# The program's block is opened without the drain of GpSimd at its end

## The chip, the cores and the metric

The kernel runs on one core of one Trainium2 chip. A core has five engines with instruction streams of their own: TensorE (PE), VectorE (DVE), ScalarE (ACT), GpSimd (POOL) and SyncE (SP). They meet only at semaphores. Sixteen DMA engines move data between HBM and the on-chip memory; here they are fed from the queues of SP, ACT and POOL. The metric is the device time of one execution in microseconds (us), lower is better.

## What is computed

The reference is two layers of a graph network on 50,000 nodes of 128 features with 12,500 edges. Cut to what matters:

```
# layer 0: max over the edges that enter a node
e      = x[src] * (1 + softplus(c) * edge_weight)
pooled = relu(layer_norm(e @ pool_w + pool_b))
agg    = max(segment_max(pooled, dst), 0)
h      = relu(layer_norm(concat(x, agg) @ final_w + final_b))
x      = layernorm(x + h)
# layer 1: relational convolution, 8 bases, mean over the edges
msg    = x[src];  coeff = comp[edge_type]
agg_b  = segment_sum(msg * coeff[:, b], dst) / max(deg, 1)     # b = 0..7
out    = concat(agg_0..agg_7, x) @ weight + bias
x      = layernorm(x + out)                                     # the result
```

## The kernel before

The edges are sorted by destination and padded to 98 tiles of 128. The nodes are worked on in 98 groups of 4 x 128 rows, then 25 further groups take up the nodes that have edges. Two loops, unrolled, run on all engines.

The first loop (`step`, up to about 645 us of the trace) makes the dense part of both layers. SP loads and stores whole groups; GpSimd adds a bias row (L436), gathers source and destination rows by index, scales the source rows, and in its last part scatters the corrected rows of layer 0 into the table `x1_table` (L406 and L413 are the helpers `indirect` and `gather`, which issue all indirect DMAs).

The second loop (`step_c`, 25 units of up to four edge tiles) makes the edge part of layer 1: GpSimd gathers four tiles of rows, TensorE and VectorE form the products and segment sums, ScalarE scales the result (L810), and GpSimd scatters it into the output, 98 indirect DMAs in all. A unit's scatters are issued five units behind its gather (`OUT_LAG`), so the last five units of GpSimd's stream hold no gathers, only scatters. After the loop GpSimd waits until all scatters have landed (L493 and L494: one wait for each of the four semaphores `out_scattered`). These are its last instructions inside its body.

The order of the instructions is that of the code; no scheduler moves anything.

Of the kernel before, what the change touches and what calls it, by code (L numbers as in the profile page):

```python
# [71 lines left out]
def gnn_kernel(nc, x, src_cols, dst_cols, dst_next_cols, dst_rows, dst_prev_rows, type_line,  # L72
# [34 lines left out]
    with ExitStack() as ctx:  # L107
# [166 lines left out]

            return x1[:, g % 2, m, :] if g < DENSE else agg_all[:, (g - DENSE) * CH + m, :]

        block = ctx.enter_context(nc.Block())  # L277

        @block.sync  # L280
# [1003 lines left out]
```

How the kernel before makes its waits and increments, by code:

```python
def need(eng, sem, count):  # L47
    if isinstance(count, int) and count <= 0:
        return
    eng.wait_ge(sem, count)
# [13 lines left out]
    def need(self, at):  # L65
        self.eng.wait_ge(self.sem, at)
# [239 lines left out]
            def coef_load(q):  # L306
                r = q * PAIR // (TYPE_TILES * LINE_BLOCKS)
                sp.wait_ge(line_stored[r], 16 * len(blocks_of(r)))
                used = q - COEF_SLOTS
                if used >= 0:
                    sp.wait_ge(S["dve_prod"], products_upto(used * PAIR // UNIT, 1, used % (UNIT // PAIR)))
                sp.dma_start(coefs[:, q % COEF_SLOTS, :, :, :].rearrange("p t b e -> p (t b e)"),
                             coef_line[q * PAIR:(q + 1) * PAIR].rearrange("(o t) b e -> o (t b e)", o=1)
                             .broadcast_to([P, PAIR * NB * P])).then_inc(coefs_in[q % COEF_SLOTS], 16)
# [1 line left out]
            def step(s):  # L316
                c = s
                b = c % 2
                if c == 2:
                    sp.wait_ge(S["mask_made"], 1)
                    sp.dma_start(mask_line.rearrange("o (t e) -> (o t) e", e=P), same_rows[:, :]).then_inc(S["mask_stored"], 16)
                if c == 4:
                    sp.wait_ge(S["mask_stored"], 16)
# [6 lines left out]
                    t = c - LATE  # L330
                    slot = t % SLOTS
                    sp.wait_ge(dst_in[slot], 16 * (t // SLOTS + 1))
                    sp.dma_start(x_dst_table[:, bass.ds(t * D, D)], x_dst[:, slot, :]).then_inc(dst_stored[slot], 16)
```

## Time and profile before

| | us |
|---|---|
| median of three runs | 912.48 (911.65 to 912.67) |
| the profiled execution, its own time | 910.83 |
| its span, first to last instruction of the program | 909.0 |
| GpSimd busy | 717.8 |
| TensorE, VectorE, ScalarE busy | 769.2, 777.6, 610.0 |

The profile is of one execution. Its page gives busy time by engine, the span in 40 slices (each digit tenths of a slice), the DMA queues, and the chain of work that ended last.
### The profile page before, as it was taken

Reading aid. Unit: us, or ns where it says so; the run is one execution under the profiler, and the core shown is the slowest. Engines: PE = TensorE matmul, PEld = TensorE weight load, DVE = VectorE, ACT = ScalarE, POOL = GpSimd, SP = SyncE. Lnnn points to the kernel's source line nnn. Section 1 sums busy time; section 2 is a strip of 40 time slices with the busy share of each in tenths; the row PEclk is TensorE's granted clock in tenths of the full one; section 3 lists DMA queues with packets and bytes.
Section 4 is the critical chain, followed back from the end, with each engine's and each line's share of the span. In section 5 each row is a group of like instructions: output and inputs, shape, how many; then the busy total and the mean of one; then the engine's idle time right before and its main releaser. Section 6 shows DMA issues by size and latency. Waiting matters only on the chain. (4 is left out here: it accounts for less than half of the span.)

```text
span 909.0 us, 18559 instructions
## 1 busy us (share of the span) xinstructions
PE 769.2 (85%) x4588; PEld 566.3 (62%) x4588; DVE 777.6 (86%) x2823; ACT 610.0 (67%) x2862; POOL 717.8 (79%) x702
## 2 busy tenths in 40 slices
PE   5699999999999999999999988777299998988920
PEld 3577777777777777777778777666144444444410
DVE  6889999999999999999999979887179999989940
ACT  3799999999999999999999867776201111111120
POOL 2588888988989898898898667777777777777774
PEclk9999999999999999999999989999799999999975
DMA  4377676666666666666666422334188888877610
GB/s 114 111 230 236 193 234 209 197 213 206 207 199 215 205 201 207 208 205 198 203 205 200 123 67 86 101 107 177 46 293 272 304 295 286 300 276 286 230 47 27
DMA packets 88576, 175.46 MB, mean 193 GB/s; under 512 B 16716, under 2 KB 34024, under 8 KB 82199
## 3 DMA queue, kind: packets, MB, share of 16 engines
q1 hardware_dynamic: 71286, 144.02, 46.7%
q0 software_dynamic: 15744, 29.71, 10.8%
q8 instruction: 38, 0.62, 0.3%
q10 hardware_dynamic: 1440, 0.56, 0.2%
q14 instruction: 68, 0.55, 0.2%
HBM read 105.88 MB, written 70.88 MB: 194 GB/s over the span
## 5 line engine op out<-in xcount | busy, mean ns | idle before, releaser
L704 ACT ACTIVATE junk<-ps 128x128 bf16<-128x128 f32 x884 | 235.1, 301 | 30.1 <-PE ps L554 19.3
L704 ACT ACTIVATION_READ_ACCUMULATOR junk<-ps 128x1 f32 x884 | 206.7, 235 | 0.0
L656 PE MATMUL ps<-agg_all,w_cen 128*128 128x512 f32 (+1 forms) x400 | 176.0, 593 | 5.9 <-DVE agg_all L1185 5.1
L406 POOL DMA_INDIRECT x_dst<-in_x,dst_i x98 | 153.9, 1571 | 17.6 <-issue 7.7
L551 PE MATMUL ps<-w_cen,xT 128*128 128x128 f32 x984 | 160.2, 295 | 0.0
L436 POOL TENSOR_TENSOR work<-work,vec_raw 128x512 f32<-128x512 f32 x98 | 127.8, 1304 | 30.4 <-DVE work L1084 29.7
L551 PEld LDWEIGHTS ps<-w_cen,xT 128*128 128x128 f32 x984 | 129.9, 197 | 28.9 <-issue 28.9
L1185 DVE TENSOR_TENSOR agg_all<-coefs,ps 128x1024 f32<-128x1024 f32 x98 | 117.7, 1210 | 31.6 <-PE ps L642 18.3
L1084 DVE SCALAR_TENSOR_TENSOR work<-ps,st,vec_raw 128x128 f32<-128x128 f32 x492 | 137.8, 343 | 0.4 <-ACT st L719 0.3
L1016 DVE BATCH_NORM_STATS2 bn<-work 128x6 f32<-128x128 f32 x492 | 135.2, 280 | 1.2 <-DVE st L1004 0.6
L406 POOL DMA_INDIRECT x_table<-agg_all,scat_i x98 | 104.9, 1070 | 37.7 <-issue 28.3
L524 PE MATMUL ps<-w_cen,work 128*128 128x128 f32 x984 | 132.5, 279 | 0.0
L656 PEld LDWEIGHTS ps<-agg_all,w_cen 128*128 128x128 f32 x400 | 75.2, 193 | 91.3 <-issue 90.9
L743 ACT ACTIVATE work<-work,st 128x128 f32<-128x128 f32 x294 | 126.4, 525 | 0.6 <-DVE st L1072 0.6
L524 PEld LDWEIGHTS ps<-w_cen,work 128*128 128x128 f32 x984 | 122.1, 195 | 0.1
L406 POOL DMA_INDIRECT out_rows<-work,scat_i x98 | 97.4, 994 | 29.9 <-issue 29.2
L413 POOL DMA_INDIRECT rows<-in_x,src_i x98 | 95.4, 973 | 29.9 <-issue 29.6
L413 POOL DMA_INDIRECT rows<-x_table,src_i x98 | 93.5, 954 | 31.8 <-issue 29.6
L805 ACT ACTIVATE st<-st 128x4 f32<-128x4 f32 x25 | 5.1, 205 | 163.4 <-DVE st L1221 163.1
L537 PE MATMUL ps<-ident,rows 128*128 128x128 f32 x590 | 89.1, 282 | 19.4 <-ACT xT L764 8.7
L537 PEld LDWEIGHTS ps<-ident,rows 128*128 128x128 f32 x590 | 70.4, 146 | 24.3 <-ACT xT L764 11.0
L1030 DVE SCALAR_TENSOR_TENSOR work<-work,rows 128x512 f32<-128x512 f32 x123 | 84.6, 688 | 0.0
(139 smaller groups left out, 1371.9 us busy)
## 6 DMA issues: line engine op xcount, KB each, us to landing
coefs<-coef_line SPq DMA_DIRECT2D x49, 1024.0 KB, 6.0
rows<-in_x SPq DMA_DIRECT2D x97, 256.0 KB
x_table<-work SPq DMA_DIRECT2D x97, 256.0 KB
out_rows<-outb SPq DMA_DIRECT2D x97, 256.0 KB
x_dst_table<-x_dst SPq DMA_DIRECT2D x98, 64.0 KB
rows<-x_dst_table SPq DMA_DIRECT2D x24, 256.0 KB
same_prev<-mask_line SPq DMA_DIRECT2D x7, 224.0 KB, 4.1
x_dst<-in_x,dst_i POOLq DMA_INDIRECT x98, 4.0
```

The source lines that it names most:

```text
L406: return pool.indirect_dma_start(*args, bounds_check=last_node, oob_is_err=False)
L413: return pool.indirect_dma_start(rows_of, None, table, by(columns, t))
L436: pool.tensor_tensor(h, h, vec_raw[:, BET_F:BET_F + 1, :].broadcast_to([P, CH, D]), ALU.add).then_inc(S["pool_b"], 1)
L524: last = pe.matmul(Y[b][:, cols(m, m + 1)], x1T[:, b, m, :], w_cen[:, W_ROOT, :], start=True, stop=True, skip_group_check=True)
L537: last = pe.transpose(XT[:, cols(m, m + 1)], rows[:, slot, m, :], ident[:, :])
L551: last = pe.matmul(H[1 - b][:, cols(m, m + 1)], xT[:, 1 - b, m, :], w_cen[:, W_TOP, :], start=False, stop=is_dense(c, 1), skip_group_check ...
L656: last = pe.matmul(MT[b][:, 0:n * D], w_cen[:, W_BASE + m, :], prod[:, b, m, 0:n, :].rearrange("p t d -> p (t d)"), start=(m == 0), stop=( ...
L704: last = nc.scalar.activation(junk[:, kind * CH + m, :], bank[:, cols(m, m + 1)], ACT.Square, accum_out=power[:, b, 1, TOP + kind * CH + m ...
L743: last = nc.scalar.activation(x1_tile(c - 4, m), hn[:, (c - 4) % SLOTS, m, :], ACT.Identity, bias=st[:, 3, TOP + m:TOP + m + 1], scale=st[ ...
L1016: own.mark(dve.bn_stats(bn[:, RES + m, :], hn[:, (c - 3) % SLOTS, m, :]))
L1084: last = dve.scalar_tensor_tensor(hn[:, (c - 2) % SLOTS, m, :], H[b][:, cols(m, m + 1)], st[:, 7, TOP + m:TOP + m + 1], vec_raw[:, GAM_F, ...
L1185: dve.tensor_tensor(prod[:, b, half, two, :], coefs[:, p % COEF_SLOTS, :, half, :].rearrange("p t m d -> p m t d"), GX[c % len(GX)][:, col ...
```

## The change

The block is opened with a flag that leaves the DRAIN of GpSimd out of the barrier at its end.

```
-        block = ctx.enter_context(nc.Block())
+        block = ctx.enter_context(nc.Block(no_gpsimd_drain=True))
```

No instruction in the five bodies changes, and none changes its place. In the barrier behind them, by the instructions of the two programs:

- GpSimd: the DRAIN is gone. What is left is the EVENT_SEMAPHORE that waits until `gather` is 4 and the one that sets `release`.
- TensorE, VectorE, ScalarE, SP: the DRAIN stays but signals nothing; behind it stands one more EVENT_SEMAPHORE each, which adds one to `gather`, and then the wait for `release` as before.

The barrier ahead of the bodies keeps all its DRAINs. The waits at L494 stay.

## Rows read from the trace of the kernel before

**Rows 1.** The page: span, busy time by engine, the span in 40 slices.

```profile
span 909.0 us, 18559 instructions
...
PE 769.2 (85%) x4588; PEld 566.3 (62%) x4588; DVE 777.6 (86%) x2823; ACT 610.0 (67%) x2862; POOL 717.8 (79%) x702
...
POOL 2588888988989898898898667777777777777774
PEclk9999999999999999999999989999799999999975
DMA  4377676666666666666666422334188888877610
```

**Rows 2.** Busy time by stretch (us from start to end, length, busy by engine; clock, DMA).

```profile
core 0: us, PE busy (x) PEld busy (x) DVE busy (x) ACT busy (x) POOL busy (x), PEclk, DMA share, GB/s
693.00:850.00 157.00, 144.79 (x429) 70.21 (x428) 150.32 (x333) 26.91 (x91) 119.60 (x123) 0.99 0.82 292
850.00:880.00 30.00, 19.79 (x68) 11.13 (x68) 21.33 (x69) 7.41 (x25) 23.00 (x24) 0.90 0.29 102
880.00:899.90 19.90, 0.00 (x0) 0.00 (x0) 0.00 (x0) 0.69 (x2) 14.29 (x15) 0.50 0.14 45
899.90:909.00 9.10, 0.00 (x0) 0.00 (x0) 0.00 (x0) 0.00 (x0) 0.00 (x0) 0.50 0.00 0
```

**Rows 3.** Chain that ended last, 893 to 910 us: start, length, what.

```profile
894.69 0.30 issue
894.99 0.98 POOL out_rows L406
895.98 0.30 issue
...
897.31 0.26 issue
897.57 0.98 POOL out_rows L406
```

**Rows 4.** Scatters to the output from 880 us on: duration ns, starts, issue to landing.

```profile
L406 POOL DMA_INDIRECT out_rows<-work,scat_i x15: 982/982/984, 879.6 to 897.6; - x15
...
DMA to landing us min/median/max: 2.2/2.3/2.3
```

**Rows 5.** Source line L107, closing barrier: duration ns min/median/max, first and last start us.

```profile
L107 POOLq EVENT_SEMAPHORE  x2: 17/17/17, 908.9 to 908.9; - x2
L107 SPq DRAIN  x1: 128/128/128, 848.6 to 848.6; - x1
L107 PEldq DRAIN  x1: 487/487/487, 870.1 to 870.1; - x1
L107 DVEq DRAIN  x1: 203/203/203, 874.7 to 874.7; - x1
L107 ACTq DRAIN  x1: 674/674/674, 881.9 to 881.9; - x1
L107 POOLq COMPARE_BRANCH  x1: 41/41/41, 899.8 to 899.8; - x1
L107 POOLq DRAIN  x1: 8887/8887/8887, 899.9 to 899.9; - x1
L107 SPq EVENT_SEMAPHORE  x1: 17/17/17, 909.0 to 909.0; - x1
...
L107 PEldq EVENT_SEMAPHORE  x1: 51/51/51, 909.0 to 909.0; - x1
```

**Rows 6.** Source line L1273, opening barrier, same columns.

```profile
L1273 POOLq DRAIN  x1: 187/187/187, 0.3 to 0.3; - x1
...
L1273 SPq EVENT_SEMAPHORE  x1: 17/17/17, 0.7 to 0.7; - x1
```

**Rows 7.** Timeline of the start: start us, length, engine, line, operation, tiles.

```profile
1.29 0.73 POOL L385 DMA_DIRECT2D src_i<-in_src_cols  x1 [0.84 <-POOLq L1273]
...
4.24 0.29 POOL L399 TENSOR_SCALAR_AFFINE_SELECT ident<-pooled 128x128 f32<-128x128 f32 x1 [0.17 <-POOL rel_row L396]
...
5.20 0.71 PEld L537 LDWEIGHTS ps<-ident,rows 128*128 128x128 f32 x4 [5.20 <-POOL ident L399]
```

## The prediction

> **What bounds the kernel now.** I read the page first, then the end of the trace by stretches, then the chain, then the line of the closing barrier. The page shows three engines with much work over the span (VectorE 86%, TensorE 85%, GpSimd 79%), and GpSimd's row alone keeps its digits to the last slice [rows 1]. For a change that touches only the end of the program the averages say little; what matters is who comes last. The stretches say it: up to 850 us all of them work, between 880.0 and 899.9 us TensorE and VectorE do nothing, ScalarE has 0.69 us, and GpSimd has 15 scatters; from 899.9 to 909.0 us every engine has 0.00 us busy and the DMA engines move 0 GB/s [rows 2]. The chain gives the same order: GpSimd issues one scatter after another, 0.98 us each with 0.30 us of issue between them, the last from 897.57 us on [rows 3].
>
> The chain stops at 898.55 us (897.57 + 0.98), yet the span is 909.0 us. The 10.4 us between are of the kind that the chain leaves out, a sequencer's own. The view of line L107 has them [rows 5]: GpSimd's branch out of its body at 899.8, its DRAIN from 899.9 with 8887 ns, its two EVENT_SEMAPHOREs at 908.9, and the releases of the other engines at 909.0. The other four had come to their DRAINs between 848.6 and 881.9 us and been done after 674 ns at the most, so nobody is waited for but GpSimd. Two things bound the last 30 us, then: first GpSimd's issue of scatters, and behind it one DRAIN of 8.89 us that stands alone on the path.
>
> What does this DRAIN wait for? Not for data: the scatters land 2.2 to 2.3 us after their issue [rows 4], so the last has landed at about 897.57 + 2.2 = 899.8 us, and it is this landing for which L494 had GpSimd wait before the branch. Nor, as far as rows can tell, for a backlog of descriptors that GpSimd still had to write: then landings would fall behind the issues more and more, and over 15 scatters in a row they stay between 2.2 and 2.3 us. It is work, or polling, that the profile doesn't resolve. The DRAIN in the opening barrier, with four small memsets before it and no DMA, took 187 ns [rows 6].
>
> **The change part by part.**
>
> *The DRAIN of GpSimd goes.* 1 x 8.887 us [rows 5], alone on the path. Once it is gone, the next thing late is still GpSimd: its EVENT_SEMAPHORE finds the four arrivals in `gather` long made (the latest, ScalarE's, at 881.9 + 0.67 = 882.6 us, 17.3 us before), sets the release, and the others follow within 0.1 us, as they do now between 908.9 and 909.0. Bound from both sides: -8.89 us if nothing behind takes the work over, 0 if all of it comes back outside the program (first rival), and a gain beyond 8.89 us has no row for it, since the EVENT_SEMAPHOREs stay.
>
> *The other four engines get one EVENT_SEMAPHORE more each.* Such instructions take 17 ns on SP, 51 ns on TensorE [rows 5]. They lie at 849 to 883 us under the scatters of GpSimd, which run until 899.9 us. Cost nothing; the cover is 17 us thick. If it were gone, the dearest, ScalarE's or TensorE's, would add 0.02 to 0.05 us.
>
> *GpSimd's waits at L494* stay, so the output has landed before the barrier in both versions. The branch at 899.8 us stays as well.
>
> *The rest of the trace*, all up to 899.9 us, has the same instructions in the same order: cost 0. Runs differ by themselves (911.65 to 912.67 us, so -0.83 and +0.19 around the median).
>
> Sum, against the profiled execution: span 909.0 - 8.89 = 900.15 us, own time 910.83 - 8.89 = **901.94 us**. That execution lies 1.65 us under the median of the three runs, so for the median I take the same difference: 912.48 - 8.89 = **903.59 us**, that is -0.97%.
>
> The point that the sum rests on is what the time counts outside the span. The profiled execution's time is 1.83 us longer than its span (910.83 - 909.0), so something around the program is counted, at its start or at its end, and no row shows what. Of 8.89 us of another flush there is no room in it now, but before the change GpSimd has just been flushed when the program ends.
>
> On this the Trainium skill has a rule that speaks against the change. "VectorE: DVE Perf Modes", section "The DRAIN you can't avoid", says that the runtime puts DRAINs of its own before and behind a program, on all five engines, about 12 ns each. By this a DRAIN of GpSimd would follow the program anyway, and one that is 12 ns behind a flushed GpSimd need not be so behind one that is not; taken so, the sum would be 0 instead of -8.89 us. No row here shows an instruction outside the program. "Runtime: NRT & Kernel Launch", section "The ~15µs preamble/postamble breakdown", gives about 1.5 us to the barrier behind a program and 1.5 us to the reset of semaphores; 1.83 us of this trace is of that size, so part of it may be counted.
>
> **The rivals.**
>
> *The flush moves behind the program (no change).* What GpSimd has to finish after its indirect DMAs is finished at the point where somebody next needs the engine empty. If that is part of what follows the program and the time counts it, the DRAIN's 8.89 us come back there; some of it can run beside what lies in the 1.83 us. Time: 912.48 - 8.89 + 8.89 = 912.48, down to 910.7 if all of the 1.83 us hides it. For it: the DRAIN waits for neither data nor a backlog, which looks like a fixed duty that somebody must do; the time does count more than the span. Against it: 1.83 us is little, and that an ending needs the engine empty is shown nowhere; the DRAIN may be such a duty only because it is asked for. The same result would come if the flush fell to the next execution's opening DRAIN (187 ns now): GpSimd makes `ident` at 4.24 us, for which the first weight load waits until 5.20 us [rows 7], so 8.7 us there would be on the path in full.
>
> *It moves in part.* The work runs by itself from 899.9 us, and what comes behind meets only the rest, or only one half of the flush is needed: between 905 and 910 us, middle 907.5.
>
> *It is paid twice (slower).* If more than one point outside asks GpSimd to be empty, one behind the program and one at its start, and each finds the queue unflushed, each pays 8.89 us: 912.48 - 8.89 + 2 x 8.89 = 921.4 us. It decides from the second payment on; with one it is the rival above. Against it: an engine that has been flushed once answers a second time quickly, as the 1.83 us after the present DRAIN show, so the second would need new work in between, and there is none but the next execution's memsets.
>
> *The flag does nothing.* Excluded: the two programs differ by exactly this DRAIN and the four semaphore instructions.
>
> **How the numbers follow.** The forecast with the full gain: 0.62. It has the one row that is as plain as a row can be, an 8.9 us instruction alone on the path at the very end. The flush moved whole: 0.27, since the only doubt is outside the trace, and the trace gives the DRAIN nothing to wait for that would go away by itself. In part: 0.06. Twice: 0.05, with any other way to be slower.
>
> The predicted time is that of the likeliest, 903.6 us; its own range is 902.7 to 904.3 us (the spread of the runs on both sides, and 0.5 us for the barrier's new form). With 0.62 this is not yet 8 in 10, so the range reaches to the case of no change with its spread: 902.6 to 912.8 us, 0.62 + 0.27 + 0.06, less what falls over the edges, some 0.85; it can't be narrower, as the two cases lie at its ends. A measurement of this kernel tells 0.2% (1.8 us) from no change. Faster: 0.62 + 0.06 and a few of the moved case in which the 1.83 us hide it, less what is lost, makes 0.68. Within 0.2%: 0.26. Slower: 0.06.
>
> **What would show it.** In the changed kernel's profile, line L107 has no DRAIN of GpSimd, two EVENT_SEMAPHOREs of GpSimd at 899.9 to 900.1 us, and the releases of the other four at about 900.1; the span is 900.0 to 900.3 us. This part is close to certain (if everything up to 899.9 us repeats). What decides is the execution's own time against its span: 1.8 us more, as now, for the forecast; about 10.7 us more for the first rival with the flush at the end; and for a flush at the start a DRAIN at L1273 of some 9 us in place of 187 ns, and a span that is again 909. The prediction would be wrong as a whole if the time stayed at 912 with a span of 900, and wrong in its reading of the DRAIN if anything before 899.9 us moved.

## The result and the profile after

| | kernel before | changed kernel |
|---|---|---|
| median of four runs, us | 912.58 (911.65 to 914.93) | 903.98 (900.03 to 904.34) |
| ratio, with its 95% interval | | 0.9889 (0.986 to 0.9918) |
| the profiled execution: own time, span | 910.83, 909.0 | 903.88, 902.1 |

The change makes the kernel faster by 1.1% (0.8 to 1.4). The median came out at 903.98 us where 903.6 was forecast; the ratio says a little more than that, 0.9889 x 912.48 = 902.35 us, which lies 0.25 us under the lower end of the range. The section on where the prediction was right and where it failed comes back to it.

First the view of the closing barrier's line in the changed kernel, which answers to [rows 5] (columns: duration in ns min/median/max, first and last start in us):

```profile
L107 SPq EVENT_SEMAPHORE  x2: 17/17/17, 852.4 to 902.0; - x2
L107 PEldq EVENT_SEMAPHORE  x2: 51/51/51, 872.4 to 902.0; - x2
...
L107 ACTq EVENT_SEMAPHORE  x2: 17/17/17, 884.6 to 902.0; - x2
L107 POOLq EVENT_SEMAPHORE  x2: 17/17/17, 901.9 to 902.0; - x2
...
L107 ACTq DRAIN  x1: 686/686/686, 883.9 to 883.9; - x1
L107 POOLq COMPARE_BRANCH  x1: 41/41/41, 901.7 to 901.7; - x1
```

GpSimd has no DRAIN, and its EVENT_SEMAPHOREs stand 0.2 us behind its branch, where before 9.1 us lay between them (899.8 and 908.9). The four other engines have two EVENT_SEMAPHOREs each: the first, added one at 852 to 885 us, under the scatters of GpSimd; the second with the release at 902.0. What was to be seen at the start is there too; line L1273, as in [rows 6]:

```profile
L1273 POOLq DRAIN  x1: 187/187/187, 0.3 to 0.3; - x1
```

Busy time by stretch of the changed kernel, as in [rows 2]; the idle stretch of 9.1 us has become one of 0.4:

```profile
core 0: us, PE busy (x) PEld busy (x) DVE busy (x) ACT busy (x) POOL busy (x), PEclk, DMA share, GB/s
880.00:901.70 21.70, 0.00 (x0) 0.00 (x0) 0.00 (x0) 0.90 (x3) 15.72 (x16) 0.50 0.14 47
901.70:902.10 0.40, 0.00 (x0) 0.00 (x0) 0.00 (x0) 0.00 (x0) 0.00 (x0) 0.50 0.00 0
```

The end of the chain of the changed kernel, as in [rows 3] (start, length, what):

```profile
899.29 0.26 issue
899.55 0.98 POOL out_rows L406
```

The last scatter starts 2.0 us later than before (897.57), with the same instructions ahead of it. So this pair of profiled executions shows 6.9 us less span: 8.9 us from the DRAIN and 2.0 us lost in the body. Where the body lost them is told by the first gather of the second loop, line L413, before and after:

```profile
L413 POOL DMA_INDIRECT rows<-x_table,src_i x98: 940/945/982, 648.2 to 853.8; - x98
```

```profile
L413 POOL DMA_INDIRECT rows<-x_table,src_i x98: 940/945/982, 650.2 to 855.8; - x98
```

From this gather to the last scatter it is 249.4 us before (648.2 to 897.57) and 249.3 us after (650.2 to 899.55). The second loop repeats to 0.1 us, and the 2.0 us lie in the first loop.

The own time is 1.8 us over the span in both (910.83 - 909.0; 903.88 - 902.1), so nothing came back outside the program. This doesn't rest on one execution of each: over all executions of this and the later runs on chips where the kernel before takes about 912 us, the own time is 1.74 to 1.85 us over the span in 87 with the DRAIN, and 1.73 to 1.83 us in the 22 of the changed kernel.

### The profile page after: what moved, and what is told of

Same layout as the page of the kernel before. It is cut to its first block and busy times, and to the rows that moved or that the text cites. A ratio compares the mean times of both kernels' runs of the same rounds, so it can differ in the third digit from the quotient of the medians.

```text
span 902.1 us, 18562 instructions
## 1 busy us (share of the span) xinstructions
PE 771.0 (85%) x4588; PEld 566.9 (63%) x4588; DVE 779.1 (86%) x2823; ACT 609.9 (68%) x2862; POOL 713.0 (79%) x702
## 5 line engine op out<-in xcount | busy, mean ns | idle before, releaser
L656 PE MATMUL ps<-agg_all,w_cen 128*128 128x512 f32 (+1 forms) x400 | 179.0, 602 | 1.5 <-DVE agg_all L1185 0.9
L406 POOL DMA_INDIRECT x_dst<-in_x,dst_i x98 | 150.8, 1539 | 20.5 <-issue 7.1
L413 POOL DMA_INDIRECT rows<-in_x,src_i x98 | 95.5, 975 | 29.9 <-issue 29.6
L413 POOL DMA_INDIRECT rows<-x_table,src_i x98 | 93.5, 954 | 31.8 <-issue 29.2
```

What stands on the lines that cost most here:

```text
L406: return pool.indirect_dma_start(*args, bounds_check=last_node, oob_is_err=False)
L413: return pool.indirect_dma_start(rows_of, None, table, by(columns, t))
L656: last = pe.matmul(MT[b][:, 0:n * D], w_cen[:, W_BASE + m, :], prod[:, b, m, 0:n, :].rearrange("p t d -> p (t d)"), start=(m == 0), stop=( ...
```

## The experiments

All of them use the kernel before or the changed one with a line or two more. A DRAIN of GpSimd can be written by hand, `pool.drain()`, and has then a source line of its own.

### Is the DRAIN the whole effect?

**e1_after_again**: the changed kernel, unchanged.

> The changed kernel once more, unchanged. Theory A (the DRAIN's 8.89 us is the whole gain; what the first measurement showed beyond it, a ratio of 0.9889 or -10.1 us, is scatter of the first loop): ratio 0.9903, 8.9 us less, and the body (the start of GpSimd's branch at L107) at 899.8 us give or take 3 us, as before. Theory B (the missing DRAIN changes the body of the next execution too, by 1 us or more either way): ratio 0.989 or less, or 0.992 or more, with the branch shifted the same way in every profile without the DRAIN.

Measured: ratio 0.9885 (0.9862 to 0.9908), six runs with a median of 902.19 us. The profile's own time is again 1.8 us over its span (903.28, 901.5). The gain repeats, with theory A's 0.9903 inside the interval and B's value too. B's second condition, a shift of the body the same way in every profile, is not met: the second loop's first gather starts 2.0 and 1.2 us later than before in the first two profiles of the changed kernel (650.2, 649.4 against 648.2), and in the third, e9, 2.0 us earlier (646.2).

**e2_own_drain**: the flag stays, the DRAIN comes back by hand.

```
                 pool.wait_ge(out_scattered[j], 16 * sum(...))
+            pool.drain()
```

> The changed kernel with one DRAIN of GpSimd written out as the last instruction of its body, behind the wait for the scatters; the block's flag stays. If the DRAIN is the whole gain (A): the DRAIN takes 8.9 us, ratio to the kernel before 1.000, and the four added semaphore instructions cost nothing. If the gain came from the new form of the barrier, its waits or its signals (C): a ratio of 0.990, or a DRAIN well under 8.9 us.

Measured: ratio 0.9989 (0.9967 to 1.0011). The row of the line with the DRAIN in this kernel:

```profile
L495 POOLq DRAIN  x1: 8884/8884/8884, 898.1 to 898.1; - x1
```

With the flag and a DRAIN the gain is gone, so it is the DRAIN and not the barrier's form that makes it.

### What a DRAIN pays for

**e3_second_drain**: the kernel before with the same line added, so that two DRAINs stand in a row.

> The kernel before with a second DRAIN of GpSimd directly ahead of the block's own. If the DRAIN finishes something that is left over from the DMAs (D): the first takes 8.9 us, the second under 0.3 us, the time is 912.6. If a DRAIN has a fixed price once DMAs have been issued in the program (F): both take 8.9 us, the time is 921.4.

The two rows, of L495 and of the block's own at L107; one execution, 912.96 us:

```profile
L495 POOLq DRAIN  x1: 8884/8884/8884, 902.0 to 902.0; - x1
```

```profile
L107 POOLq DRAIN  x1: 40/40/40, 910.9 to 910.9; - x1
```

The second takes 40 ns. A DRAIN is not dear as such; it pays for something that the DMAs left and that is gone afterwards. Inside the program, then, whoever asks first pays and the next finds nothing, which speaks against the rival of a double payment.

**e4_many_drains**: the kernel before with DRAINs at five more places (the comments are added here).

```
+            pool.drain()                      # after the two index loads
             last_node = pool.to_reg(N - 1)
...
                 b = s % 2
+                if s in (10, 30):
+                    pool.drain()
...
+            pool.drain()                      # between the loops
             def gather_x1(q):
...
                 pool.wait_ge(out_scattered[j], 16 * sum(...))
+            pool.drain()
```

> The kernel before with DRAINs of GpSimd at five more places: behind the two plain loads at the start (landed), at steps 10 and 30 of the first loop, between the loops (all scatters landed; 242 indirect DMAs after the one before), and directly ahead of the block's own. If the price goes by the DMAs since the last DRAIN (D, 8887 ns for 490 indirect ones, 18 ns each): about 0.1 us, 0.2, 0.9, 4.4, 3.6 us and under 0.3 us for the block's own. If it is one price for any DRAIN with DMAs since the last (G): 8.9 us at each of the first five, under 0.3 us at the last. If it is a price per DRAIN (F): 8.9 us at all six. The time grows by what they sum to, less what the slack of GpSimd in the first loop hides.

The rows of GpSimd's DRAINs, from five source lines; the third line holds steps 10 and 30:

```profile
L402 POOLq DRAIN  x1: 223/223/223, 7.7 to 7.7; - x1
```

```profile
L433 POOLq DRAIN  x2: 5657/7250/8843, 48.9 to 149.4; - x2
```

```profile
L474 POOLq DRAIN  x1: 8619/8619/8619, 656.5 to 656.5; - x1
```

```profile
L499 POOLq DRAIN  x1: 8857/8857/8857, 917.4 to 917.4; - x1
```

```profile
L107 POOLq DRAIN  x1: 46/46/46, 926.3 to 926.3; - x1
```

None of the three theories holds. It is no fixed price (0.22 and 0.05 us exist), and it is not in proportion (244 DMAs cost 8.62 us, 196 cost 8.86; in the order of the program it is 244 since the DRAIN at step 30, all of them indirect, where the expectation says 242). The two inside the first loop can't be read as a price. GpSimd still worked on instructions ahead of them: its last one ended at 52.3 us under the DRAIN from 48.9 to 54.6, and at 154.2 us under the one from 149.4 to 158.2. What is left behind these ends, 2.3 and 4.0 us after 10 and 40 DMAs, can still hold the landing of the last transfers, which no row separates (timeline of GpSimd: start us, length, line, operation):

```profile
51.88 0.41 POOL L428 TENSOR_TENSOR rows<-rows,e_scale 128x128 f32<-128x128 f32 x1
54.62 1.27 POOL L439 TENSOR_TENSOR work<-work,vec_raw 128x512 f32<-128x512 f32 x1 [2.32 <-DVE work L1089]
```

So the 0.57 us a DMA that the next expectation takes from the 5.66 us is not a price.

**e5_late_drain** and **e6_idle_drain**: is it a backlog that GpSimd would work off by itself, or does the DRAIN start the work? In the first a long memset lies between the last landing and the DRAIN, in the second GpSimd waits idle for three loads of SyncE. Neither changes the result; both write buffers that are no longer read.

```
+            pool.memset(agg_all[:, 0:TILES, :], 0.0).then_inc(S["const_ready"], 1)
+            pool.wait_ge(S["const_ready"], N_CONST + 1)
+            pool.drain()
```

> The changed kernel with a memset of 128x12544 on GpSimd after all scatters have landed, then a wait for it, then a DRAIN of GpSimd. The memset overwrites a buffer nobody reads again. If the DRAIN ends something that GpSimd's cores are still busy with from the last DMAs (backlog, H): the memset starts some 8.9 us late or the DRAIN behind it takes under 0.3 us. If the DRAIN itself starts the work (I): the memset starts within 0.3 us of the branch-free end of the waits, and the DRAIN behind it takes 8.9 us.

```
+            pool.wait_ge(coefs_in[0], 16 * (len(range(0, PAIRS, COEF_SLOTS)) + 3))
+            pool.drain()
```

> The changed kernel with three loads of 1 MB on SyncE's queue, one after the other, once all scatters have landed; GpSimd waits idle for the last of them and then has a DRAIN. The loads fill a buffer nobody reads again. Backlog (H): the DRAIN, some 15 us after the last landing, takes under 0.3 us. Work started by the DRAIN (I): 8.9 us whatever the time between.

These two and the next two ran on another chip, where the kernel before took 979.6 us instead of 912, so only durations inside their traces are used. The timeline of GpSimd in e5 and the DRAIN behind it:

```profile
971.22 0.98 POOL L406 DMA_INDIRECT out_rows<-work,scat_i  x1 [0.30 <-DMA out_rows<-work,scat_i]
973.43 10.55 POOL L495 MEMSET agg_all<- 128x12544 f32 x1 [1.22 <-DMA out_rows<-work,scat_i]
```

```profile
L497 POOLq DRAIN  x1: 8884/8884/8884, 984.0 to 984.0; - x1
```

The memset starts 2.2 us after the last scatter's issue, that is with its landing [rows 4]: no backlog is ahead of it. And a DRAIN 10.6 us later takes the same 8884 ns. In e6, the last scatter, which lands at about 969.8 + 2.2 = 972.0 us, and the DRAIN 13.6 us behind that:

```profile
969.79 0.98 POOL L413 DMA_INDIRECT out_rows<-work,scat_i  x1 [0.30 <-DMA out_rows<-work,scat_i]
```

```profile
L503 POOLq DRAIN  x1: 8884/8884/8884, 985.6 to 985.6; - x1
```

The backlog falls. Waiting does nothing to the price, so what the DRAIN does begins with the DRAIN; left out, it is not done in the time that is measured.

**e7_counted_a**, **e8_counted_b**, **e10_counted_c**, **e11_counted_d**, **e12_counted_e**: the changed kernel with DRAINs after chosen counts of scatters, each behind waits until the scatters so far have landed. The edit shown is that of e7 and e8; e10, e11 and e12 also wait there for the gathers, and e12 has a DRAIN between the loops too.

```
+                        if done * UNIT + n + 1 in DRAIN_AT:
+                            for j in range(SLOTS):
+                                need(pool, out_scattered[j], 16 * ...)
+                            pool.drain()
```

> The changed kernel with DRAINs of GpSimd in the last 18 scatters, each behind a wait until all scatters so far have landed: after scatter 80 (hundreds of DMAs before it), then 1, 2, 4 and 11 DMAs after the DRAIN before. Price by DMA with a ceiling (10 DMAs gave 5.66 us at the start, 0.57 us each; 8.9 us for 16 or more): 8.9, 0.6, 1.1, 2.3 and 6.2 us. A price for any DRAIN with DMAs since the last (G): 8.9 us five times.

> The same with DRAINs after scatters 80, 86 and 98, so 6 and 12 DMAs after the DRAIN before. Price by DMA with a ceiling: 8.9, 3.4 and 6.8 us. One price (G): 8.9 us three times.

> The changed kernel with DRAINs of GpSimd in the second loop, each behind waits until all its DMAs so far have landed: after 336 DMAs, then after 16, 32, 48 and 60 more. By 40 ns and 82 ns a DMA since the last DRAIN (1 to 12 DMAs fit it): 1.35, 2.66, 3.98 and 4.96 us; the first near the ceiling, 7.4 to 8.9 us. If the line bends before 60: less.

> The same with DRAINs after 336 DMAs, then 120 and 36 more. By the line: 36 gives 2.99 us and 120 would give 9.9 us. If there is a ceiling at about 8.9 us (no measured DRAIN is above it): 8.9 us or less for 120.

> The same with DRAINs between the loops (296 DMAs), after 40 more and after 156 more. By the line 40 gives 3.32 us. By a ceiling 296 and 156 give 7.4 to 8.9 us; by a count that starts again at zero after each 128 DMAs, 3.3 and 2.3 us.

The rows of single DRAINs, each from the line's view over a stretch that holds one. From e7, after 1, 2, 4 and 11 DMAs since the one before:

```profile
L495 POOLq DRAIN  x1: 124/124/124, 957.4 to 957.4; - x1
```

```profile
L495 POOLq DRAIN  x1: 198/198/198, 961.8 to 961.8; - x1
```

```profile
L495 POOLq DRAIN  x1: 371/371/371, 968.9 to 968.9; - x1
```

```profile
L495 POOLq DRAIN  x1: 936/936/936, 985.1 to 985.1; - x1
```

From e10, the first DRAIN (336 DMAs), then those after 32 and 60 more; from e11, after 120 more; from e12, after 156 more:

```profile
L497 POOLq DRAIN  x1: 4474/4474/4474, 708.0 to 708.0; - x1
```

```profile
L497 POOLq DRAIN  x1: 2651/2651/2651, 783.9 to 783.9; - x1
```

```profile
L497 POOLq DRAIN  x1: 4937/4937/4937, 935.4 to 935.4; - x1
```

```profile
L497 POOLq DRAIN  x1: 2656/2656/2656, 865.3 to 865.3; - x1
```

```profile
L498 POOLq DRAIN  x1: 5591/5591/5591, 916.9 to 916.9; - x1
```

All DRAINs that stood behind landed DMAs, but for e4's first (223 ns behind the two plain index loads), in one table (GpSimd issues 492 DMAs, 490 indirect and the two index loads; the last column is the duration less 43 ns, by 81.6 ns, which is the slope between 1 and 60 DMAs: (4937 - 124) / 59):

| DMAs since the DRAIN before | DRAIN, ns | as DMAs |
|---|---|---|
| 1, 2, 4, 6 | 124, 198, 371, 533 | 1, 2, 4, 6 |
| 11, 12, 16 | 936, 1017, 1349 | 11, 12, 16 |
| 32, 36, 40 | 2651, 2977, 3309 | 32, 36, 40 |
| 48, 60 | 3957, 4937 | 48, 60 |
| 120 | 2656 | 32 |
| 156 | 5591 | 68 |
| 196 (e4) | 8857 | 108 |
| 244 (e4), 296 (e12) | 8619, 8639 | 105, 105 |
| 336 (e10, e11) | 4474 | 54 |
| 474 (e7, e8) | 7414 | 90 |
| 492 (the kernel before; e2, e3, e5, e6, e15) | 8887; 8884 in each | 108 |

How the expectations did: the one price of 8.9 us (G) and the ceiling with 0.57 us a DMA, of e7 and e8, are both wrong from 1 to 12 DMAs. The line of 40 ns and 82 ns a DMA, read from these, hit all six values from 16 to 60 that e10, e11 and e12 forecast by it, to 0.03 us, and failed at 120 (2.66 us for 9.9). The ceiling missed for 336 (4.47 us where 7.4 to 8.9 were expected) and for 156 (5.59), and the count from zero after each 128 DMAs missed for 296 and 156.

Up to 60 DMAs a DRAIN costs 0.04 us and 82 ns for each DMA since the last one. Then the price falls back: 120 cost what 32 cost, and 120, 156 and 196 lie on the same line less 88 DMAs each. From 474 to 492 it rises by 18 x 81.7 ns, on the slope again. A reading that fits, and that no run shows directly: something is kept for each DMA, now and then a block of it is let go while more DMAs are issued, and a DRAIN goes through what is left, about 108 at the most in these runs. The block is not always 88. Between 336 and 474 DMAs what is left went from 54 to 90 while 138 were added, so 102 were let go there. If it happens at one fixed count of kept DMAs, the rows put this between 109 and 120: after 196 and after 492 DMAs 108 were still kept, and of 120 only 32. What fixes the point and the size of the block is open. The kernel before happened to end near the top of this sawtooth.

### Where the last microsecond comes from

**e9_after_third**: the changed kernel again.

> The changed kernel a third time, to tell the DRAIN's own 8.9 us from the spread of the first loop. If the DRAIN is the whole gain (A): a ratio of 0.9903 within its interval, and the mean of the three measurements no further than 0.1% from it. If the missing DRAIN also shortens the body (B): again about 0.9887, 10.3 us less.

Measured: 0.9894 (0.9862 to 0.9925), median 902.42 us. A's 0.9903 is inside the interval, but its second condition fails: the mean of the three ratios is 0.9889, 0.14% under it. B's value of 0.9887 is nearer.

**e13_before_again**, **e14_after_fourth**, **e15_own_drain_again**: a control, the kernel before against itself, with the changed kernel and the one of e2 on the same chip.

> The kernel before, unchanged, run as if it were a changed one, to see what the comparison itself tells of two equal programs. Ratio 1.000; if the comparison favours whatever stands second (J), about 0.999, as with the DRAIN written out by hand (0.9989).

> The changed kernel a fourth time, on the same chip as the control. DRAIN alone (A): 8.9 us under the control's own runs. Body shortened too (B): 10 us or more under them.

> The changed kernel with the DRAIN written out by hand, once more. If the barrier's new form saves something of its own (C): 1 us or more under the control's own runs. If not: within 0.7 us of them, and 8.9 us over the changed kernel.

Measured: 1.0003 (0.998 to 1.0027) for the control, 0.9878 (0.9846 to 0.991) for the changed kernel, 1.0000 (0.9975 to 1.0026) for the flag with a DRAIN by hand. The comparison has no bias that shows, and the barrier's form saves nothing that shows: e2's 0.9989 didn't come again. The changed kernel lies 10.6 us under the control by the medians (902.36, 912.94), which is what B asked for and not A; the DRAIN by hand is within 0.1 us of the control, as expected, and 10.5 us over the changed kernel where 8.9 was expected.

What the runs with one and the same kernel show is how wide they scatter. Over all executions on chips where the kernel before takes about 912 us: kernel before 55 runs, mean 912.76 us, 906.44 to 918.20; control 12 runs, mean 913.01; with the DRAIN by hand 24 runs, mean 912.18; changed kernel 22 runs, mean 902.48, 899.83 to 905.29. The difference of the means is 912.76 - 902.48 = 10.3 us against the kernel before and 912.18 - 902.48 = 9.7 us against the flag with a DRAIN, with an error of 1.0 and 1.4 us (standard deviations of 1.8, 2.3 and 2.9 us by the root of the counts, added in squares and doubled). The DRAIN explains 8.9 of it. The rest is 1.4 us, with an error of 1.0, in the first comparison and 0.8 us, with an error of 1.4, in the second; all 91 runs with a DRAIN at the end against the 22 without give 10.2 us with an error of 0.9. So a further gain of about 1 us is likely and not shown beyond doubt, as each of the four ratios has 0.9903 in its interval, though all four lie under it. The profiled executions don't show it in the body, and four against four that differ by up to 5 us couldn't: the first gather of the second loop starts at 650.2, 649.4, 646.2 and 649.5 us in four of the changed kernel (mean 648.8) and at 648.2, 651.3, 646.6 and 646.9 us in two with the block's DRAIN and two with one by hand (mean 648.3). Whether a queue left unflushed, or 8.9 us less of idling, helps the next execution's first loop a little stays open.

## Where the prediction was right, and where it failed

- **The DRAIN alone on the path, 8.89 us.** Right. It is gone from L107, the EVENT_SEMAPHOREs follow the branch by 0.2 us, and with a DRAIN put back by hand the gain is gone (0.9989 and 1.0000). The difference of the predicted and measured medians is 0.4 us, and that it is so small is luck: the same kernel's other three medians are 902.19, 902.42 and 902.36 us. (The sum for the span has a slip, 909.0 - 8.89 is 900.11 and not 900.15; nothing rests on it.)
- **The added EVENT_SEMAPHOREs cost nothing, under 17 us of cover.** Right: they stand at 852 to 885 us, 17 us ahead of GpSimd's arrival (901.9), and e15 against e13, 912.86 to 913.01 us in the mean, shows no price. Nor could it show one of 0.05 us; that it is nothing is read from the rows.
- **The DRAIN waits neither for data nor for a backlog.** Right, and e5 and e6 show it where the prediction had only the landings: the same 8884 ns after 10.6 us of other work and after 13.6 us of waiting. What it was left with, work or polling that someone must do, is now a price by the DMA, 82 ns each, for what is still kept. What the engine does in this time stays open.
- **The flush moves behind the program (0.27).** Didn't happen. The own time stays 1.8 us over the span, where this rival needed 10.7, and the DRAIN at L1273 still takes 187 to 189 ns in the four profiles of the changed kernel. No later execution pays either: the 22 runs lie between 899.83 and 905.29 us, and 8.7 us more in any of them would show. In the time that is measured the duty existed only because it was asked for; whether anything is done about the queue between two executions, no row shows. The Trainium skill's rule of runtime DRAINs on all five engines behind a program ("VectorE: DVE Perf Modes", "The DRAIN you can't avoid") cannot be seen in these traces; if there is one on GpSimd, it lies outside what the time counts or doesn't flush this queue.
- **In part, twice.** Neither happened; in e3 a second DRAIN right behind the first takes 40 ns, which speaks against a second payment without new DMAs between.
- **The body repeats at cost 0, with a spread of -0.83 and +0.19 us.** This is the step that failed: the term for the rest of the trace was put at 0 with a spread of about 1 us, and the ratio puts the gain at 10.1 us (912.48 - 902.35), 1.2 us more than the DRAIN's 8.89. The spread was read from three runs. The unchanged kernel scatters over 906.4 to 918.2 us in 55 runs, with a standard deviation of 2.3 us, and all of it visible in the profiles lies in the first loop: the second loop began between 646.2 and 651.3 us in profiles of the same body. Two means of four such runs each differ by up to 2.9 us from this alone (standard deviations of 2.3 and 1.8 us, worked as above), and the interval of the ratio came out at 0.3% on either side, not the 0.2% that the prediction gave a measurement. The lower end of the range, 902.6 us, allowed 1.0 us under the forecast, where 2 to 3 were due; and the 0.8 to 1.4 us of gain beyond the DRAIN lie on that side. Their cause, if they are more than scatter, stays open.

## What to carry to other kernels

The DRAIN of GpSimd at the end of this program cost 8.9 us behind 492 DMAs. It stands in no list of busy time, and is found only by the view of the barrier's line or by the gap between the chain's end and the span. Where the kernel itself waits for every DMA of GpSimd to land, as here, it is worth trying to leave it out. How much there is to gain can't be read from the number of DMAs beyond 60: here a DRAIN cost 4.9 us after 60, 2.7 us after 120 and 8.9 us after 196. These counts begin at an earlier DRAIN of the same program; no run had another program. And three runs that lie within about 1 us are no measure of a kernel's spread.

## What the runs showed of the hardware

- A DRAIN of GpSimd behind DMAs that have landed takes 0.04 us and 82 ns for each DMA since the last DRAIN, measured from 1 to 60; behind no DMA 40 to 46 ns.
- More DMAs can mean a cheaper DRAIN: 60 cost 4.9 us, 120 cost 2.7 us, 156 cost 5.6 us, 196 cost 8.9 us; no DRAIN behind landed DMAs took more than 8.89 us. Where the price falls back, GpSimd's stream shows no gap: in the kernel before all 196 DMAs of the second loop start 1.24 to 1.34 us after the one before.
- The price doesn't shrink with time: 10.6 us of memset and 13.6 us of waiting left the 8884 ns as they were.
- Leaving the DRAIN out at the end of the program had no price that shows in 22 executions of the changed kernel: 1.73 to 1.83 us outside the span, as with it.
